# Three narrowings of VectorE walk their tiles in steps of 128 elements

## What is computed

```python
h = relu(LN(x));  x = x + attention(h, adj)     # scores masked where adj <= 0
h = relu(LN(x));  x = x + mlp((1 + eps) * h + adj @ h)
h = relu(LN(x));  x = x + adj @ (h @ W) + b
h0 = h = relu(LN(x))
A = (adj != 0)
for l in range(5):
    agg = A.T @ (h @ weight[l])
    r = sigmoid(agg @ w_ir + h @ w_hr + b);  z = sigmoid(agg @ w_iz + h @ w_hz + b)
    n = tanh(agg @ w_in + b_in + r * (h @ w_hn + b_hn))
    h = (1 - z) * n + z * h
x = x + h * mask
```

## Time and profile before

| | us |
|---|---|
| median of 3 runs | 709.81 (708.55 to 710.15) |
| the profiled execution, its own time | 708.05 |
| its span, first to last instruction | 705.9 |
| TensorE busy in it | 660.1 (94%) |
| VectorE busy | 601.6 (85%) |
| ScalarE busy | 524.4 (74%) |
| GpSimd busy | 401.1 (57%) |

### The profile page before, as it was taken

How to read it: one execution, slowest core, us unless ns; L and a number is a source line. 1 busy time by engine, 2 the same in 40 slices (tenths; PEclk the granted TensorE clock), 3 DMA queues, 4 the chain that set the end, 5 groups by cost and what they waited for, 6 DMA issues and landing times.

```text
span 705.9 us, 13197 instructions
## 1 busy us (share of the span) xinstructions
PE 660.1 (94%) x4380; PEld 430.2 (61%) x4380; DVE 601.6 (85%) x1360; ACT 524.4 (74%) x962; POOL 401.1 (57%) x357
## 2 busy tenths in 40 slices
PE   3899999999999999974899999999999999999995
PEld 2678888888888888752455555555555545545552
DVE  3777877777877777666699999999999999999996
ACT  2678888888888888723588888777787777777774
POOL 4656666666666666521255555555555555555554
PEclk9999999999999999985899999999999999999998
DMA  5111111111111100000333333333333334333332
GB/s 154 31 32 31 31 32 31 32 32 31 31 31 31 31 17 2 2 0 2 64 65 64 62 61 60 74 73 68 71 62 74 75 75 75 61 76 73 68 70 74
DMA packets 114690, 35.82 MB, mean 51 GB/s; under 512 B 87680, under 2 KB 114624, under 8 KB 114624
## 3 DMA queue, kind: packets, MB, share of 16 engines
q1 hardware_dynamic: 113424, 34.79, 23.0%
q10 hardware_dynamic: 1200, 0.20, 0.2%
HBM read 9.80 MB, written 4.19 MB: 20 GB/s over the span
## 4 chain that ended last, share of the span: by engine, by line
DVE 36%; issue 10%; PE 3%; POOL 2%; ACT 1%; DMA 0%; DVEq 0%; POOLq 0%; SPq 0%
DVE h_parts L1297 12%; DVE cand L1304 7%; DVE t_parts L1289 6%; DVE r L1308 5%; DVE new L1293 4%; PE psum L50 3%; POOL h0T L1264 2%; DVE out L1280 2%; DMA h_nodes<-h_parts 0%; DVE h_parts L1299 0%; DVEq L1307 0%; ACT cand L1241 0%; POOLq L1046 0%; ACT t_parts L1233 0%; PE psum L1193 0%
## 5 line engine op out<-in xcount | busy, mean ns | idle before, releaser
L50 PE MATMUL psum<-h_parts,gru_w 128*128 128x512 f16 x720 | 185.1, 382 | 6.3 <-DVE out L1280 3.9
L1264 POOL TENSOR_TENSOR h0T<-cand,zh 128x512 f32<-128x512 f32 x80 | 101.6, 1270 | 143.4 <-DVE cand L1304 143.4
L50 PE MATMUL psum<-t_parts,gru_w 128*128 128x512 f16 x720 | 181.5, 379 | 0.0
L50 PEld LDWEIGHTS psum<-h_parts,gru_w 128*128 128x128 f16 x720 | 69.8, 98 | 91.9 <-issue 10.8
L1258 POOL TENSOR_TENSOR zh<-z,h0T 128x512 f32<-128x512 f32 x80 | 101.7, 1271 | 25.8 <-ACT z L1236 25.8
L50 PEld LDWEIGHTS psum<-t_parts,gru_w 128*128 128x128 f16 x720 | 66.9, 98 | 66.4 <-DVE t_parts L1289 2.9
L1233 ACT CAST t_parts<-psum 128x512 f16<-128x512 f32 x80 | 46.8, 585 | 72.6 <-PE psum L50 72.6
L1297 DVE CAST h_parts<-h0T 128x512 f16<-128x512 f32 x80 | 90.1, 1126 | 4.9 <-PEq L380 4.8
L578 POOL TENSOR_TENSOR prob<-prob,row_max 128x512 f32<-128x512 f32 x64 | 68.7, 1086 | 20.0 <-DVE row_max L956 18.7
L1241 ACT ACTIVATE cand<-new,gates_b 128x512 f32<-128x512 f32 x80 | 65.0, 812 | 7.4 <-DVE new L1293 7.3
L1236 ACT ACTIVATE z<-psum,gates_b 128x512 f32<-128x512 f32 x80 | 62.2, 778 | 5.9 <-PE psum L50 0.9
(11 more groups left out here) (131 smaller groups left out, 1202.5 us busy)
## 6 DMA issues: line engine op xcount, KB each, us to landing
x_all<-in_x SPq DMA_DIRECT2D x16, 256.0 KB, 3.2
adj<-in_adj SPq DMA_DIRECT2D x16, 256.0 KB, 2.8
out_x<-out SPq DMA_DIRECT2D x16, 256.0 KB, 2.3
h_nodes<-h_parts SPq DMA_TRANSPOSE x80, 3.1
gw<-in_L_gnn_weight SPq DMA_DIRECT2D x1, 320.0 KB, 5.7
W<-in_L_gnn_W SPq DMA_DIRECT2D x2, 128.0 KB, 4.4
wi<-in_L_gnn_w_ih SPq DMA_DIRECT2D x1, 192.0 KB, 5.7
wh<-in_L_gnn_w_hh SPq DMA_DIRECT2D x1, 192.0 KB, 4.4
```

The lines of the kernel that those rows point to most:

```text
L50: return nc.tensor.matmul(out, lhsT, rhs, start=start, stop=stop)
L1264: pool.tensor_tensor(state(now), by_graph(cand[now.s][:, :]), by_graph(zh[now.s][:, :]), ALU.add)\
```

## The change

`by_node` swaps the two inner dimensions of an access pattern. Source and destination of the three narrowings are given through it, so an instruction goes through 128 nodes outside and, at each, through the 4 graphs inside. Neighbours in that order lie 128 elements apart: 512 bytes in the float32 source, 256 bytes in the 16-bit destination. Each element is still written to the place where it was written before. The instructions that the three are in order with, their semaphores and all other code stay as they are: on every engine the same instructions stand in the same order, and on VectorE the three forms are 128x128x4 instead of 128x512.

```diff
+def by_node(x):
+    return x.rearrange("p g n -> p n g")
...
-                v.tensor_scalar(gone[group.odd][:, :, :], adj[group.odd][:, :, :], 0.0, MASKED, ALU.is_le, ALU.mult)\
+                v.tensor_scalar(by_node(gone[group.odd][:, :, :]), by_node(adj[group.odd][:, :, :]), 0.0, MASKED,
+                                ALU.is_le, ALU.mult)\
                     .then_inc(gone_ready, 1)
...
-                v.tensor_scalar(t["edges"][:, group.all, :], adj[group.odd][:, :, :], 0.0, None, ALU.not_equal)\
+                v.tensor_scalar(by_node(t["edges"][:, group.all, :]), by_node(adj[group.odd][:, :, :]), 0.0, None,
+                                ALU.not_equal)\
                     .then_inc(edges_ready, 1)
...
-                    v.tensor_copy(by_graph(hp[s][:, 0, :]), state(now)).then_inc(hi_ready, 1)
+                    v.tensor_copy(by_node(by_graph(hp[s][:, 0, :])), by_node(state(now))).then_inc(hi_ready, 1)
                     dve.wait_ge(hi_ready, now.count)
                     v.tensor_tensor(by_graph(hp[s][:, 1, :]), state(now), by_graph(hp[s][:, 0, :]), ALU.subtract)\
                         .then_inc(lo_ready, 1)
```

## The result

The changed kernel takes 770.11 us in the median of 4 runs (769.37 to 771.98), against 709.86 for the kernel before on the same chip: a ratio of 1.0857, 95% interval 1.0831 to 1.0882. That is 60.2 us more, where 17 were forecast, and it lies above the range. The profiled execution took 770.78 us, its span 768.6. In the profile after, line 1297 is line 1303, 1299 is 1305, 1289 is 1295, 1293 is 1299, 1304 is 1310, 1308 is 1314, 1258 is 1264, 1264 is 1270, 1236 is 1242, 940 is 944, 945 is 950 and 951 is 957.

The account below looks back on a forecast made before the run. TensorE was taken to pace the GRU slot, the VectorE and GpSimd loop just inside it. GRU narrowings 17.4 us plus first stage 0, on 708.05 profiled, gave 725.5; 1.8 more to the median gave 727 us, range 708.5 to 762.

Parts of the forecast that it names:

- What bounds the kernel: GRU slot: TensorE paces at 4.33 us; the VectorE and GpSimd loop takes 4.32, about 0.01 us cover.
- The wait behind zh: GRU slot: the two-at-a-time narrowing of h waits for GpSimd's product zh and ends 0.28 us after it.
- the size of x: Extra time of one 512-element narrowing: one more 1.05 ns cycle on each of 256 steps, 0.27 us.
- The upper bound from the reciprocal's row: Narrowing's extra time at most 0.96 us, from 3.75 ns per element in the reciprocal of 16 sums.
- The count of 67 slots: GRU: 67 of 80 slots pay x - 0.01, 17.4 us; 12 finished-group slots absorb up to 0.44, one is lost filling.
- The first stage: Mask and edges, 16 times each: hidden in VectorE's 1.49 us idle, 0 us; at x = 0.96 some 7 us.
- The 1.98 ns of the Trainium skill: Narrowing: 1.98 instead of 1.05 ns on 256 steps would add 0.24 us, the sum 2 us lower.
- Free hops: Rival for the narrowings: x = 0, mode stays, no change at 709.8 us; chance 0.10.
- a lost mode with free hops: Rival: narrowing one at a time, 0.68 us, without waiting for GpSimd; 704.6 us; lost mode's chance 0.12 overall.
- the wait at the finished groups: TensorE in the GRU: some 0.4 us of wait at each of 13 finished groups could be won.
- a second cycle on each step: Lost-mode case: second cycle on each of 512 steps, narrowing 1.22 us, 710 to 711 us; unchanged 0.04 of 0.12.
- The clock: Rival: TensorE's idle time in GRU slots drops its clock from 2.4 to 1.2 GHz, over 737 us; chance 0.04.

Follow-up runs that it names:

- e5: Kernel before, with the narrowing of h hopping 128 elements only in its source, written contiguously (wrong order): 720.11 us, ratio 1.0163.
- e6: Kernel before, with the narrowing of h reading contiguously and hopping 128 elements only in its 2-byte destination (wrong order): 768.36 us, ratio 1.0848.
- e4: Kernel before plus a block behind its end timing 22 narrowing forms alone, then five with GpSimd busy; no whole timing; hopping float16 destination, contiguous source 1304 ns.
- e9: Changed kernel, with the narrowing of h as a one-at-a-time maximum over one element on the same walk: 806.68 us, ratio 1.1378 to the kernel before.
- e2: Changed kernel with only the state's narrowing put back, so only mask and edges hop: 710.03 us, ratio 1.0016 to the kernel before.
- e7: Kernel before, with the narrowing of h as a one-at-a-time maximum over one element, no hops: 703.78 us, ratio 0.9933.

## Why the prediction was wrong

**What bounds the kernel** was right. TensorE's loop of 4.33 us and VectorE's and GpSimd's of 4.32 lay as close as read: e5 lengthens the second by 0.18 us behind zh and the slot by 0.17. The wait behind zh stays, as said, and zh follows h0T by 1.23 us now.

**The failed step is the size of x:** "I take one more cycle a step, 1.05 ns ... x = 256 x 1.05 = 0.27 us." It measures 0.89 us, so a step takes 4.5 ns and not 2.1, and by e6 the destination alone accounts for it: a 2-byte element that is written alone in its piece of 16 bytes holds its step for 4.4 ns. The value was about right for the wrong tile: between float32 tiles the same walk costs 0.293 us (e4, line 1403), and the source's side of the real one 0.25 (line 1393). I had asked what a hop costs and never what a 2-byte element costs that is written alone, though the narrowing is just that. The upper bound from the reciprocal's row, 0.96 us, was close, but I set it aside for its division and for PSUM, and ended the range at x = 0.8. With no row for the write side, the range had no business ending inside its own bounds. That the bound came near is no merit of it: it took its 3.75 ns from reads of PSUM, and those cost nothing in e4 (a hopping PSUM source into a contiguous tile takes 691 ns, as a contiguous one does).

**The count of 67 slots** nearly held: 67 x (0.89 - 0.01) = 59 us, against 60.2 measured, and 67 x 0.17 = 11.4 against 11.3 in e5. The prediction had let each finished group absorb up to 0.44 us. The starts of the narrowings show what it does: the short slot behind a finished group is 4.09 us before and in e5, so there it absorbs the delay whole. In the changed kernel it is 4.42, so 0.33 us come back 12 times, 4 us, of which the next slot gives back 0.1 each time (4.44 to 5.21). From the first narrowing to the last the two traces differ by 60.8 us. In e9, with 1.21, nothing is absorbed.

**The first stage** was put at 0 for 0.27 us and at 7 us for 0.96. It cost about 1.1 us at 0.9 (e2). The bound added both delays in full behind the edges, but of the mask's 0.89 us only 0.15 are left where the edges are issued, and with the edges' 1.28 the sum just fits the 1.49 us.

**The rules weighed.** The Trainium skill's rule that the two-port mode asks for SBUF on both sides and an even outermost count (or an odd one that is the same on both sides), but not for a unit step (Vector Engine (DVE) Microarchitecture Reference, section 5.1), holds here: the changed walk waits for GpSimd, its steps of 4.5 ns carry two elements, and the walk of 7 x 73 into 511, odd and unequal, loses the mode. The 1.98 ns of the Trainium skill, same page, section "Measured stream behaviour on trn2", were for 4-byte words, and for those the runs come near (0.24 us worked out, 0.293 measured). For 2-byte destinations the measurement is 4.4 ns, and decides.

**The rivals.** Free hops are excluded by e5 and e6. The mode is not lost by this walk. What the prediction worked out for a lost mode with free hops, 704.6 us, e7 shows as 703.8, and by the mechanism that was named, the wait at the finished groups. With the hops it is 806.7 (e9), where the prediction had put 710 to 711 for a second cycle on each step. The clock stayed at 1.00 in the stretch shown, with TensorE busy 87% of it.

## What to carry to other kernels

Look at the destination first when an access pattern is turned: a 2-byte or 1-byte element written alone costs 4.4 ns a step where a 4-byte one costs about 2, and two neighbouring float16 elements that fill a 4-byte word at each stop cost nothing. So give a transposing walk an inner run that fills a word, or else let the source do the hopping: it cost 11 us here instead of 60. And a narrowing that runs two elements a step may lose more by waiting for GpSimd than it wins by the mode: here the one-at-a-time form, slower by itself (0.68 against 0.42 us), made the kernel 5 us faster.

## What the runs showed that was not expected

- The loss for single 16-bit writes goes by pieces of 16 bytes: 452, 736, 1299 ns for steps of 4, 8 and 16 bytes, and no more beyond (1304 at 256).
- It is much alike on three engines. For 512 elements VectorE needs 1.74 us more one at a time (0.69 to 2.43), and GpSimd (0.61 to 2.46) and ScalarE (0.61 to 2.47) 1.85 us more, the source's hops included.
- A hopping source in PSUM costs VectorE nothing (691 and 691 ns), a hopping float32 source in SBUF 0.25 us.
- A hopping read that has waited for GpSimd costs 0.18 us instead of the 0.25 it costs alone; the hopping write costs its full 0.89 either way.
